# Picking's masks made in place in a ring of three banks, with search, queries and twelve weighings placed anew

## What is computed

```
q = (x @ Wq).reshape(b, n, 8, 64) * 64 ** -0.5
kv_scores, indices = _pk(x, Wq_pk, pk_keys)     # top 16 of 16 x 16 candidates of two top-16 lists
k = sum over the 16 of kv_scores * keys_table[indices]
v = sum over the 16 of kv_scores * values_table[indices]
out = causal softmax attention of q, k, v over 8 heads, then @ Wo
```

## Time and profile before

| | |
|---|---|
| time, median of 3 runs | 6943.39 us (6937.87 to 6958.16) |
| time of the profiled execution | 6937.05 us |
| its span | 6935.2 us |
| granted TensorE clock over the span | 0.983 |
| PE busy | 6277.6 us (91%) |
| POOL busy | 4397.3 us (63%) |
| ACT busy | 4668.2 us (67%) |
| DVE busy | 4120.9 us (59%) |

### The profile page before, as it was taken

The page is one execution under the profiler, slowest core; times in us unless marked ns, Lnnn a source line. Parts: engine busy times, 40 slices in busy tenths (PEclk is TensorE's granted clock), DMA queues, the critical chain, the costliest instruction groups (busy, mean ns, idle before and its releaser), DMA issues.

```text
span 6935.2 us, 87978 instructions
## 1 busy us (share of the span) xinstructions
PE 6277.6 (91%) x28800; PEld 3567.8 (51%) x28800; DVE 4120.9 (59%) x13328; ACT 4668.2 (67%) x10873; POOL 4397.3 (63%) x4108
## 2 busy tenths in 40 slices
PE   2799999999999999999999999999999999999977
PEld 1455555555555555555555555555555555555533
DVE  7564847647484764748575574757557475752147
ACT  0676777767677776767676777767777776767733
POOL 0575857758585775858576585857668585766600
PEclk9999999999999999999999999999999999999978
DMA  1111111111111111111111111111111111111100
GB/s 33 43 49 38 46 42 43 48 37 48 38 49 39 45 47 37 49 36 49 39 46 45 37 49 36 52 36 46 46 36 49 38 51 37 46 47 43 44 19 15
DMA packets 93493, 290.94 MB, mean 42 GB/s; under 512 B 17879, under 2 KB 26546, under 8 KB 92780
## 3 DMA queue, kind: packets, MB, share of 16 engines
q1 hardware_dynamic: 92748, 285.25, 12.4%
q10 hardware_dynamic: 288, 0.07, 0.0%
HBM read 280.68 MB, written 4.61 MB: 41 GB/s over the span
## 4 chain that ended last, share of the span: by engine, by line
PE 71%; POOL 12%; ACT 10%; DVE 6%; issue 2%; DMA 0%; SPq 0%; DVEq 0%; ACTq 0%
PE accu L520 29%; POOL dense_w L451 12%; PE dense L527 8%; PE dense L506 7%; PE dense L508 7%; PE sims L638 3%; PE work L644 2%; ACT past L910 2%; PE work L631 1%; PE work L566 1%; PE sims L608 1%; PE work L684 1%; PE dense L492 1%; ACT dense_w L905 1%; PE work L618 1%
## 5 line engine op out<-in xcount | busy, mean ns | idle before, releaser
L451 POOL TENSOR_TENSOR dense_w<-dense_w,store 128x375 f32<-128x375 f32 x4096 | 4394.9, 1088 | 2208.8 <-ACT dense_w L905 2126.5
L520 PE MATMUL accu<-dense_w,store 128*128 128x375 f32 x8192 | 3284.0, 484 | 151.7 <-POOL dense_w L451 101.0
L910 ACT ACTIVATE past<-dense 128x375 bf16<-128x375 f32 x4096 | 1982.5, 484 | 1118.3 <-PE dense L527 1090.0
L905 ACT ACTIVATE dense_w<-dense 128x375 f32<-128x375 f32 x4096 | 1966.8, 480 | 177.2 <-PE dense L508 172.2
L520 PEld LDWEIGHTS accu<-dense_w,store 128*128 128x128 f32 x8192 | 1408.5, 190 | 473.7 <-POOL dense_w L451 125.7
L527 PE MATMUL dense<-store,hot 128*128 128x375 bf16 x4096 | 1326.2, 324 | 116.8 <-ACT past L910 115.7
L506 PE MATMUL dense<-store,spread 96*128 96x375 bf16 x4096 | 1335.9, 326 | 25.5 <-ACT dense_w L905 25.4
L508 PE MATMUL dense<-past,far 128*128 128x375 bf16 x4096 | 1329.5, 325 | 0.0
L527 PEld LDWEIGHTS dense<-store,hot 128*128 128x128 bf16 x4096 | 394.8, 96 | 955.3 <-ACT past L910 813.5
L506 PEld LDWEIGHTS dense<-store,spread 96*128 96x128 bf16 x4096 | 399.8, 98 | 714.1 <-issue 323.1
L508 PEld LDWEIGHTS dense<-past,far 128*128 128x128 bf16 x4096 | 405.7, 99 | 228.4 <-issue 13.4
(11 more groups left out here) (255 smaller groups left out, 6499.5 us busy)
## 6 DMA issues: line engine op xcount, KB each, us to landing
store<-in SPq DMA_DIRECT2D x513, 512.0 KB, 3.3
x_in<-in SPq DMA_DIRECT2D x16, 187.5 KB, 2.4
store<-in SPq DMA_DIRECT2D x1, 2048.0 KB, 9.1
queries_kept<-n3T SPq DMA_DIRECT2D x16, 93.8 KB, 3.6
h_saved<-h SPq DMA_DIRECT2D x16, 93.8 KB
store<-queries_kept SPq DMA_DIRECT2D x16, 93.8 KB, 2.5
store<-h_saved SPq DMA_DIRECT2D x16, 93.8 KB
out<-store SPq DMA_DIRECT2D x16, 93.8 KB
```

The costliest lines, as they stand in the source:

```text
L451: nc.gpsimd.tensor_tensor(dense_w[:, i % RING, :], dense_w[:, i % RING, :], first_of[:, i // CHUNKS, :], ALU.mult).then_inc(s["weighed"], 1)
L520: last = mm(accu[:, 0, 0:S], table[:, n % PIECE_RING, i % PIECE, :], dense_w[:, i % RING, :], start=(c == 0), stop=(c == CHUNKS - 1))
L905: fn(dense_w[:, i % RING, :], dense[:, n % 2, 0:S], ACT.Relu).then_inc(s["taken"], 1)
L910: fn(past[:, j % 2, :], coded, ACT.Relu).then_inc(s["past"], 1)
```

## The change

- **Masks in place, three banks.** The far product, `far` and `past` are gone. Each step has one bank of a ring of three from its hot product on. ScalarE's mask multiplies by 1024 and writes into the bank it read; the spread product, with a negated `spread`, accumulates onto it; ScalarE's keep takes `Relu` of minus the bank. The factors use the same ring. The wait for a free bank stands before the hot product now, for the bank's user three items ago.
- **Search on row halves.** `simw` holds the second key half's 512 columns on partitions 64 to 127, `n2T` is copied twice, and the second product of `similarities` runs on array rows 64 to 127.
- **Scores and queries over 128 rows.** `qT` and `wq_s` get zeros in rows 64 to 127; `scores` and `queries` contract over 128 rows. `queries(h + 2)` stands after the first 5 slots of a head, directly ahead of `mix(h - 1)`; ScalarE's `scale_q(h + 2)` stands after the exponentials.
- **Twelve weighings on VectorE.** Steps 161, 163, ..., 183 (`DIRECT`): no keep and no weighing on GpSimd; VectorE takes min(bank, 0) times `minus_first` out of the bank into `dense_w`. `weigh_direct(b - 1)` stands at the end of VectorE's `ahead(b)`, behind `pick_rows(b, 1)`; for the last element, ahead of its attention. `minus_first` costs ScalarE one more copy for each element.

```diff
+BANKS = 3
+LAST_STRETCH = EARLY + AHEAD - FILL_SECOND[2]
+DIRECT = [i for i in range(STEPS) if LAST_STRETCH <= i < LAST_STRETCH + FILL_SECOND[2] - SUM_LAG and i % 2 == 1]
...
-            def bank_free(n):
-                if n >= 2:
-                    pe.wait_ge(s["taken"], n - 1)
-                return dense[:, n % 2]
+            def bank_free(b, n):
+                if n >= BANKS:
+                    kind, what = ORDER.items[n - BANKS]
+                    if kind == "step" and what in DIRECT:
+                        pe.wait_ge(s["direct"], b * len(DIRECT) + DIRECT.index(what) + 1)
+                    elif kind == "step":
+                        pe.wait_ge(s["taken"], passed(what) + 1)
+                    else:
+                        pe.wait_ge(s["factor_kept"], (b * H + what[0]) * FACTORS + what[1] + 1)
+                return dense[:, n % BANKS]
...
-                    to = bank_free(ORDER.spread[i])
-                    if j > STEPS:
-                        pe.wait_ge(s["past"], i + 1)
-                    mm(to[:, 0:S], spread[0:3 * I1S, c % (CHUNKS // GROUPS), :], second_of[0:3 * I1S, c // (CHUNKS // GROUPS), h, :],
-                       start=True, stop=False)
-                    mm(to[:, 0:S], far[:], past[:, i % 2, :], start=False, stop=True).then_inc(s["spread"], 1)
+                    pe.wait_ge(s["past"], i + 1)
+                    mm(dense[:, ORDER.step[i] % BANKS, 0:S], spread[0:3 * I1S, c % (CHUNKS // GROUPS), :],
+                       second_of[0:3 * I1S, c // (CHUNKS // GROUPS), h, :],
+                       start=False, stop=True, skip_group_check=True).then_inc(s["spread"], 1)
...
-                    if j >= 1:
-                        pe.wait_ge(s["past"], j)
-                    mm(coded, hot[:, j % CHUNKS, :], ranksT[:, j // CHUNKS, :], start=True, stop=True).then_inc(s["coded"], 1)
+                    if j % CHUNKS == 0:
+                        pe.wait_ge(s["factor_kept"], (b * H + j // CHUNKS + 1) * FACTORS)
+                    to = bank_free(b, ORDER.step[j])
+                    mm(to[:, 0:S], hot[:, j % CHUNKS, :], ranksT[:, j // CHUNKS, :], start=True, stop=True,
+                       skip_group_check=True).then_inc(s["coded"], 1)
...
                 for c in range(2):
-                    last = mm(sims[0:P, c, :], n2T[:, tile(t)], simw[:, c * 512:(c + 1) * 512], start=True, stop=True)
+                    half = slice(c * D, (c + 1) * D)
+                    last = mm(sims[0:P, c, :], n2T[half, tile(t)], simw[half], start=True, stop=True)
...
-                    fn(dense_w[:, i % RING, :], dense[:, n % 2, 0:S], ACT.Relu).then_inc(s["taken"], 1)
+                    fn(dense_w[:, i % RING, :], dense[:, ORDER.step[i] % BANKS, 0:S], ACT.Relu, scale=-1.0).then_inc(s["taken"], 1)
...
-                    fn(past[:, j % 2, :], coded, ACT.Relu).then_inc(s["past"], 1)
+                    here = dense[:, ORDER.step[j] % BANKS, 0:S]
+                    fn(here, here, ACT.Relu, scale=FAR).then_inc(s["past"], 1)
...
+            def weigh_direct(b):
+                for n, i in enumerate(DIRECT):
+                    if n == 0:
+                        dve.wait_ge(s["factor_kept"], (b * H + DIRECT_HEADS[-1] + 1) * FACTORS)
+                    dve.wait_ge(s["spread"], i + 1)
+                    v.scalar_tensor_tensor(dense_w[:, i % RING, :], dense[:, ORDER.step[i] % BANKS, 0:S], 0.0,
+                                           minus_first[:, DIRECT_HEADS.index(i // CHUNKS), :], ALU.min,
+                                           ALU.mult).then_inc(s["direct"], 1)
...
                 for _ in pick_rows(b, 1):
                     pass
+                weigh_direct(b - 1)
```

More of the change, by code:

```diff
@@ L65, with passed @@
 assert sum(PICKS_INSIDE) == PIECES_SOON
+LAST_STRETCH = EARLY + AHEAD - FILL_SECOND[2]
+DIRECT = [i for i in range(STEPS) if LAST_STRETCH <= i < LAST_STRETCH + FILL_SECOND[2] - SUM_LAG and i % 2 == 1]
+DIRECT_HEADS = sorted({i // CHUNKS for i in DIRECT})
+def passed(i):
+    return i - sum(d < i for d in DIRECT)
+BY_POOL = passed(STEPS)
 class Schedule:
     def __init__(self):
-        self.spread, self.factor = {}, {}
+        self.step, self.factor = {}, {}
         items = [("factor", (0, k)) for k in range(FACTORS)]
         for j in range(SLOTS):
-            if 0 <= j - SPREAD_LAG < STEPS:
-                items.append(("spread", j - SPREAD_LAG))
             if self.factor_at(j) is not None:
                 items.append(("factor", self.factor_at(j)))
+            if j < STEPS:
+                items.append(("step", j))
         for n, (kind, what) in enumerate(items):
-            (self.spread if kind == "spread" else self.factor)[what] = n
-        self.items = len(items)
-        assert self.items % 2 == 0
+            (self.step if kind == "step" else self.factor)[what] = n
+        self.items = items
+        assert len(items) % BANKS == 0
     @staticmethod
@@ L194, in tower @@
         h1 = sb("h1", [P, NT, D])
-        n2T = sb("n2T", [D, S])
+        n2T = sb("n2T", [128, S])
         s16 = sb("s16", [P, 2 * H, K])
@@ L495, in factor @@
                                   start=True, stop=True)
-                last.then_inc(s["spread"], 1)
+                last.then_inc(s["factored"], 1)
             def dense_slot(b, j):
@@ L630, in queries @@
                 def queries(h):
-                    mm(work[0:D, 0, 0:S], wq_s[:, h], n2T_now, start=True, stop=True).then_inc(s["q_mm"], 1)
+                    mm(work[0:D, 0, 0:S], wq_s[:, h], halves[:, S:2 * S], start=True, stop=True).then_inc(s["q_mm"], 1)
                 def scores(h):
@@ L637, in scores @@
                     for i, dst in enumerate((sims[0:P, 0, 0:P], sims[0:P, 0, P:S], sims[0:P, 1, 0:S])):
[L638 removed]
+                        last = mm(dst, qT[:, h % 2, tile(i)], kvT[:, h, 0:(i + 1) * P], start=True, stop=True)
                     last.then_inc(s["s_mm"], 1)
@@ L875, in keep @@
                 nc.scalar.copy(h1_now[:], h1[:])
-                nc.scalar.copy(n2T_now, n2T[:]).then_inc(s["kept"], 1)
+                nc.scalar.copy(n2T_now, n2T[0:D]).then_inc(s["kept"], 1)
             slot = [0]
@@ L950, in prepare @@
                 act.wait_ge(s["nT_mm"], b * 2 + 2)
-                nc.scalar.copy(n2T[:], work[0:D, 1, 0:S]).then_inc(s["nT_done"], 1)
+                nc.scalar.copy(n2T[0:D], work[0:D, 1, 0:S])
+                nc.scalar.copy(n2T[D:128], work[0:D, 1, 0:S]).then_inc(s["nT_done"], 1)
             def keep_similarities(b, t):
@@ L996, in attention @@
                         exponentials(h + 1)
+                    if h + 2 < H:
+                        scale_q(h + 2)
                     if h == 3 and soften_next is not None:
@@ L1590, in tables @@
     row, key, chunk = np.arange(128)[:, None, None], np.arange(128)[None, None, :], np.arange(CHUNKS // GROUPS)[None, :, None]
-    spread = np.where(row < 3 * I1S, row % I1S == 2 * chunk + key // SUB, False).astype(f).reshape(128, CHUNKS // GROUPS * 128)
+    spread = -np.where(row < 3 * I1S, row % I1S == 2 * chunk + key // SUB, False).astype(f).reshape(128, CHUNKS // GROUPS * 128)
     return [rope, decay, mask, np.eye(128, dtype=f), iota, runs, keys, hot, spread]
```

64 lines of the change are left out of this document (32 added, 32 removed).

## The result

The changed kernel takes 6757.41 us (median of 3 runs, 6750.01 to 6759.06) against 6943.39: the ratio is 0.9725 [0.9699, 0.9751]. The forecast was 6730, with 6600 to 6840 as its range: the right direction and inside the range, some 30 us too low. The profiled execution has a span of 6757.3 us, and 6759.06 us as its own time.

The account below looks back on a forecast made before the run. The prediction took PE's queue as the bound, except where picking waits for POOL's weighing. From 6937 us, attention -280, `ahead` +86 and the last element -18 gave 6725; against the median 6730, range 6600 to 6840.

Parts of the forecast that it names:

- A plain slot of 0.95 us: Plain slots on PE: dropping the far product's 0.16 us shortens a slot from 1.11 to 0.95 us.
- The rival that the mask in place takes too long: ScalarE's mask and keep need 1.11 us instead of 0.76, so slots stay at 1.11: 7133 us; chance 5%.
- Attention -17.5 us: Each attention: 12.5 us from the far product plus 6.3 from scores and queries, less 1.3; 16 times, -280 us.
- the margin of 1.3: Attention: 1.3 us taken off the gain for heads in which VectorE comes late once heads are shorter.
- The rival that the queries don't hide: Attention: queries with 128 rows don't run beside mix, so 50 us come back: 6780 us; chance 12%.
- Factor slots at 1.28 us: Slots with factors: the loop through the bank of two steps before takes 1.28 us, 0.17 more than a plain slot.
- I take nothing, as the two effects are about equal: 54 slots with factors: between a gain of 0.16 and a loss of 0.17 us, no change was counted.
- The rival that the factors' slots gain 0.16 each: Slots with factors gain like the others if ScalarE's mask ends sooner: 138 us more, 6590 us; chance 7%.
- The 75 slots, -6: Slots with nothing between them, where POOL is nearly always busy: 6 us less per element, bounds 0 and 10.
- The stall: Last 30 slots: step 164 waits for VectorE, starting 27.3 us after step 160; PE stands still over 20 us, 15 times.
- I expect part of the resumed slots at 1.2 GHz and add 2: Slots after the wait at step 164: a lower clock costs 2 us per element, bounds 0 to 5.
- The last element, -18: Last element's slots 19 to 189, without ranks beside them: 123 slots outside the factors' gain 0.16 us each, less a little.

Follow-up runs that it names:

- the fastest version: Eight single weighings on VectorE between block 1's rank operations, instead of twelve behind them in the changed kernel: 6468.63 us, ratio 0.9313.

## Why the forecast came out as it did

- **A plain slot of 0.95 us**: right (3188.67 to 3189.62). The rival that the mask in place takes too long is out: it takes 468 ns on average, no more than the 0.48 us of the earlier trace rows.
- **Attention -17.5 us**: right to the tenth in the mean, which is in part luck. Far was worth 11.8 instead of 12.5 and the tiles 6.0 instead of 6.3: 1.0 of the margin of 1.3 went there. The other 0.3 went into dips of the clock, which the prediction didn't count. Whether VectorE's lateness, the reason given for the margin, has a part in the 1.0, no run tells. The rival that the queries don't hide is out.
- **Factor slots at 1.28 us**: right in the loop, by the hot products of such slots in PE's timeline of the changed kernel:

```profile
3068.12 0.33 PE L548 MATMUL dense<-store,hot 128*128 128x375 bf16 x1 [0.15 <-ACT dense_w L926]
...
3069.41 0.33 PE L548 MATMUL dense<-store,hot 128*128 128x375 bf16 x1
...
3070.69 0.33 PE L548 MATMUL dense<-store,hot 128*128 128x375 bf16 x1 [0.15 <-ACT dense_w L926]
...
3071.97 0.33 PE L548 MATMUL dense<-store,hot 128*128 128x375 bf16 x1
```

  They stand 1.28 or 1.29 us apart. What was wrong is the term for these slots, "I take nothing, as the two effects are about equal". From the hot product of slot 30 to that of 78 an element took 84.0 us before where the clock stayed at 1.00, and takes 84.9 or 85.8 in the four elements where it does so now: the longer loop costs more than the hidden factor products give back. With the elements whose clock dips in this stage (ten of 14 after, six before) the loss is 1.5 us in the mean. The rest of the stage gained 3.5, a little more than the 3 forecast, so that the whole stage shrank by only 1.9. The rival that the factors' slots gain 0.16 each is out. By the Trainium skill (ScalarE: Activation LUTs, Step-by-step) ScalarE's way to PSUM is the quicker. The runs agree: a mask in place takes 468 ns, a keep into SBUF 479, and that is too little to lift a loop of 1.28 us to 1.11.
- **The 75 slots, -6**: right (-5.7), as a choice between bounds of 0 and 10 rather than a sum. The slots 86 to 159 are 74; the 95.8 us of the prediction also hold the search ahead of them.
- **The stall**: right in place, cause and count (15 times, 20.8 us, releaser VectorE). Step 164 starts 26.0 us after step 160, not 27.3: the weighing takes 0.55 instead of 0.6, and the last reduction ends 25.3 us after step 160 and not 28.6, a gain of 3.2 us where 2 were taken. The prediction had set the medians of all 192 operations against the shortest times; in this stretch they took more than their medians before (2.58 and 1.84 us).
- **"I expect part of the resumed slots at 1.2 GHz and add 2"**: this term was too small. The stretch after the stall is 28.4 us, and 24.7 without it was the forecast: 3.7, of which 3.2 go away when the stall is filled with products. By the Trainium skill (TensorE: Matmul & The Clock Gate, What's actually happening) activity is what releases the throttled clock, and with 125 products in the wait the stretch behind it indeed ran at 1.00. That the whole stretch came out at 54.4 for 54.0 is luck: the stall was 1.3 too long in the forecast, what follows 1.7 too short.
- **The last element, -18**: too large together with its attention. Slots 86 to 189 gained 16.1 us (117.7 to 101.6), close to the 16.6 of 104 x 0.16. The attention and the slots up to 85 gained 12.9 (253.1 to 240.2), where 18.9 were left to gain. Of the missing 6.0, attention has 2.6 (it gained 14.9), and the slots 30 to 77, those with factors, lost 2.9 (77.0 to 79.9). Four stretches of 3.4 us at 1.2 GHz lie in the two stages after, and one before.

The 34 us by which the sum was low (6725 against 6759) are then 14 x (1.1 + 0.3 + 0.4) = 25 from the typical elements, 6.5 from the last interval, 1.8 from the one before the first attention, and 0.8 from the last attention. Of the 1.1, the slots with factors lost 1.5 and the rest of that stage gave some 0.4 more. What the prediction had at nothing is the loss in those slots and the dips of the clock outside the stalled stretch; all else came in its size or nearly.

What stays open is what starts the short clock dips inside attention and in the slots 19 to 85. They are not new: three of 14 take 153.5 instead of 150.1 us before. With the weighings between the ranks 13 of 14 take 136.0, and with the stall filled 11 of 14 take 132.3, though PE waits in the same places for the same times there. Those in attention are worth 3.7 us each, some 50 us in the fastest version. Nothing was tried against them.

## What to carry to other kernels

A transfer of work to an engine that has idle time on average is decided by that engine's queue, not by its share: weighings cost 223 us behind the ranks, nothing in an idle gap ahead of them, and gained 70 us (6538.4 to 6468.6) when laid singly between them. The numbers differ too (twelve, three and eight), but the wait of 20.8 us is for the first of the twelve alone. With a ring of few banks, one late consumer stops every engine that uses the ring: in the 21.7 us of the stall PE is busy for 1.0 us, ScalarE for 0.9, GpSimd for 2.5. And count the clock with a stall of TensorE: behind 20.8 us it cost 3 us more each time.

## What the runs showed of the hardware

- After 20.8 us without matmuls, TensorE's granted clock is 0.50 for another 6.6 us of work (6.5 to 9.0 over 14 elements); three slots take 1.85, 2.89 and 1.83 us instead of 0.95. Then it is 1.00. With 125 products in the wait it is 1.00 all along.
- Two f32 products in column halves of the array run at once with 128 and 125 contraction rows, not only with 64: they start 0.01 us apart.
- ScalarE reading and writing the same PSUM bank, 128x375 f32, takes 468 ns, against 479 from PSUM to SBUF.
- VectorE's uint16 operations of the ranks took 2.58 and 1.84 us in the mean with GpSimd busy (before, last three groups) and 2.29 and 1.22 with GpSimd standing still (the stall).
- VectorE's minimum and product of 128x375 f32, one operand in PSUM and one in SBUF, takes 549 ns; laid between other operations, a median of 537.
- The same 583 matmuls of an attention took 132.3 us at a granted clock of 1.00 and 136.0 at 0.96.
